# Edge ordering of a two-layer graph network: one-hots and payload laid out with the runs innermost, running sums by scans

## The chip, the cores and the metric

The kernel runs on one core of one Trainium2 chip. The metric is the device time of one execution in microseconds; for each kernel the median of several runs is taken. A core has the engines TensorE (PE; its weight loads are listed as PEld), VectorE (DVE), ScalarE (ACT), GpSimd (POOL) and SyncE (SP, which here issues transfers), each with a queue of its own; they wait for each other by semaphores.

## What is computed

A graph of 12,500 nodes with 128 features and 200,000 edges, sorted by destination (`dst`). First attention over the edges, then three graph convolutions with batch norms, each of which gathers a row per edge by `src`, scales it and sums it by `dst`:

```
h = relu(layernorm(x));  x = x + attention(h, src, dst, edge_attr)
h = relu(layernorm(x))
for W, b, g, beta in three layers:
    h = h @ W
    msg = h[src] * (dinv[src] * dinv[dst])[:, None]
    h = segment_sum(msg, dst) + b
    h = batch_norm(relu(h), g, beta)        # the last layer without relu
x = x + h
```

The part that the change touches computes no feature at all. It orders the edges once, so that the three layers can gather rows of `h` from on-chip memory by small matmuls.

## The kernel before

`build` (L127) calls the stages one after the other: `prepare`, `project`, `attend`, `normalise`, then `arrange` (L1355), then three times `aggregate` and `transform`. `arrange` consists of `survey` (L1381), `rank` (L1530) and `remain` (L1897). Only `rank` is changed.

`rank` takes the edges in 50 spans (`sh.SPANS`) of 28 runs (`SPAN_C`), and a run is 128 edges, one in each partition. The upper part of an edge's source index, its tile, is one of about a hundred. Each span does this:

- SyncE loads the tile numbers of its 3584 edges into `hi_bc`, the same in all partitions (L1611).
- VectorE compares them with the partition's number, `tile_hot` (L1651), which gives the one-hot `oht`. Six halvings (`halve`, L1659) add it up within each run, `count` (L1666) finishes that, and five shifted additions (`add_up`, L1676) turn it into running sums over the 28 runs, `before_c`.
- TensorE compares the edges of a run with each other in seven batches of four runs, `match` (L1810, L1815). ScalarE keeps the earlier ones (L1867). `add_ranks` (L1826, L1829) adds both kinds of count: an edge's rank within its tile.
- VectorE turns ranks into places: `take_rank` (L1683), `test`, `spill`, then five shifted additions over the runs (`run_up`, L1702) that number the edges which found no place, `spill_total` (L1708). TensorE adds the counts of the partitions ahead (`count_ahead`, L1836), ScalarE copies them, and `order_spill` (L1712) to `to_float` (L1750) end in a chunk number and a line number for every edge.
- `chunk_hot` (L1754) makes a one-hot over 29 chunks, `ohc`; `load_pay` (L1763, L1767) multiplies it with two values and a third for five of the chunks, `pay`, 63 columns a run. `line_hot` (L1777) makes the one-hot over 128 lines, `ohw`, one instruction a run.
- `put_down` (L1845) multiplies the two on TensorE, 28 matmuls of 63 columns that add up in one bank, the weights being `ohw`. ScalarE copies the result (L1882, L1884), `turn` (L1852) turns a part of it, and SyncE stores three tables.

The order on each engine is written out by hand, as a list of pairs of a lag and a step that is given to `steps` (L95): in iteration i a step with lag l works on span i - l. VectorE's list (L1793) holds steps of lags 0 to 3, with the short dependent instructions of one span placed between those of another. TensorE's list (L1856) is match 0 to 2 of a span, `count_ahead` of the one before, match 3, `turn` (lag 3), match 4 to 6, `add_ranks`, and last `put_down` with lag 2. Every dependence within an engine goes through a semaphore too. Most tiles have one buffer; `oht`, `before_c`, `tm`, `ohw`, `pay`, `placed` have two.

`pay` and `ohw` have the run as their outer dimension before (`[P, 2, SPAN_C, PAY]`, `[P, 2, SPAN_C, P]`), so a run's 63 or 128 elements are adjacent.

Of the kernel before, what the change touches and what calls it, by code (L numbers as in the profile page):

```python
# [13 lines left out]
P = 128  # L14
# [1515 lines left out]
def rank(nc, sh, env, kept):  # L1530

    with ExitStack() as c:
# [14 lines left out]
        PAD = 16  # L1547
# [4 lines left out]
        sums = [tile(f"sums{k}", [P, PAD + SPAN_C], BF16) for k in range(5)]  # L1552
# [4 lines left out]
        spills = [tile(f"spills{k}", [P, PAD + SPAN_C + 1]) for k in range(6)]  # L1557
# [10 lines left out]
        line_f = tile("line_f", [P, 2, SPAN_C])  # L1568
        ohc = tile("ohc", [P, SPAN_C, PLACE_C], BF16)
        ohw = tile("ohw", [P, 2, SPAN_C, P], BF16)  # L1570
        pay = tile("pay", [P, 2, SPAN_C, PAY], BF16)
# [10 lines left out]
        ident16, iota_col, iota_chunk = kept["ident16"], kept["iota_col"], kept["iota_chunk"]  # L1582
# [7 lines left out]
        summed = [sem(f"summed{k}") for k in range(5)]  # L1590
# [9 lines left out]
        run = [sem(f"run{k}") for k in range(5)]  # L1600
# [35 lines left out]
        @block.gpsimd  # L1636
        def _(pool):
            for k in range(5):
                nc.gpsimd.memset(sums[k][:, :], 0.0)
            for k in range(6):  # L1640
                last = nc.gpsimd.memset(spills[k][:, :], 0.0)
            last.then_inc(padded, 1)

        @block.vector
        def _(dve):
# [125 lines left out]
            def line_hot(q):  # L1771
                def go(s):
# [6 lines left out]
                    if q == 6:  # L1779
                        last.then_inc(ohw_made, 1)  # L1780
# [823 lines left out]
```

## Time and profile before

| | us |
|---|---|
| Median of 3 runs | 6932.62 (6927.31 to 6932.69) |
| The profiled execution, its own time | 6936.31 |
| Its span, first to last instruction | 6934.5 |
| PE busy | 5765.9 (83%) |
| DVE busy | 4671.8 (67%) |
| ACT busy | 2162.6 (31%) |
| POOL busy | 3099.4 (45%) |
| Ordering stage `rank`, first load to last store issued | 3320.45 to 4044.17 |

The page divides the span into 40 slices of 173 us. The ordering stage fills slices 20 to 23: there DVE's digit is 9 or 8, PE's 5 or 6, POOL's 0. In the three layers behind it PE has 9, in attention before it PE has 9 as well. A share of busy time over the whole span is an average over stages with different limits, so the stage is read by itself. TensorE's granted clock is given as a share of its full 2.4 GHz.

### The profile page before, as it was taken

The page shows a single profiled execution, that of the slowest core. Times are in us where ns is not written, and L with a number is a line of the kernel's source. Part 1 is how long each engine was busy: PE and PEld are TensorE (multiplying, and loading weights), DVE is VectorE, ACT ScalarE, POOL GpSimd, SP SyncE. Part 2 cuts the span into 40 slices and gives each one's busy share as a digit, 9 for nine tenths or more (in the row PEclk, how much of TensorE's full clock was granted, in tenths as well). Part 3 has the DMA queues.
Part 4 walks back from the last instruction along what each step waited for, and adds up shares of the span by engine and source line. Part 5 has one row for each costly group of instructions (what it writes and reads, how often), then busy time and mean ns, then how long its engine had stood idle before and what let it go on. Part 6 is the DMA issues. An engine that isn't in the chain of part 4 may idle for free. (4 is left out here: it accounts for less than half of the span.)

```text
span 6934.5 us, 161023 instructions
## 1 busy us (share of the span) xinstructions
PE 5765.9 (83%) x49778; PEld 3934.9 (57%) x49778; DVE 4671.8 (67%) x15150; ACT 2162.6 (31%) x5294; POOL 3099.4 (45%) x3151
## 2 busy tenths in 40 slices
PE   4699999999998999984566659999889999599996
PEld 2466666666666666663344436666456666366664
DVE  7455555555555555558999967777557777577776
ACT  3222222222222222223333323333443333433332
POOL 1555555555555555547000025555145555355552
PEclk9655555555555555555556679999999999799997
DMA  4333333333333333324222233333343333533335
GB/s 145 116 89 87 88 87 88 88 88 89 87 87 87 88 89 86 89 70 131 86 66 70 65 115 105 106 103 104 102 128 104 104 105 101 163 104 106 106 102 152
DMA packets 542000, 688.39 MB, mean 99 GB/s; under 512 B 217072, under 2 KB 427905, under 8 KB 541722
## 3 DMA queue, kind: packets, MB, share of 16 engines
q0 software_dynamic: 140208, 338.71, 17.1%
q1 hardware_dynamic: 401692, 348.45, 16.6%
q8 instruction: 49, 0.80, 0.0%
q14 instruction: 51, 0.42, 0.0%
HBM read 619.25 MB, written 67.52 MB: 99 GB/s over the span
## 5 line engine op out<-in xcount | busy, mean ns | idle before, releaser
L740 POOL DMA_INDIRECT at_kv<-kv_tab,at_idx x1568 | 1562.2, 996 | 1296.6 <-issue 593.6
L2250 ACT ACTIVATE ag_msg<-ag_pair 128x768 bf16<-128x768 f32 x1200 | 925.9, 808 | 1586.4 <-PE ag_pair L2180 1027.1
L2189 PE MATMUL ag_sum<-ag_hot,ag_msg 128*128 128x240 bf16 x10800 | 1300.5, 268 | 69.6 <-issue 55.5
L2189 PEld LDWEIGHTS ag_sum<-ag_hot,ag_msg 128*128 128x128 bf16 x10800 | 974.6, 98 | 443.3 <-issue 366.6
L2064 POOL DMA_INDIRECT ag_spill<-g_tab,ag_idx x600 | 580.1, 967 | 1429.5 <-DMA ag_idx<-spill_tab 777.8
L2119 DVE CAST ag_msg<-ag_pair 128x768 bf16<-128x768 f32 x600 | 572.9, 955 | 588.8 <-PE ag_pair L2180 277.2
L2180 PE MATMUL ag_pair<-xs,ag_pick 128*32 128x384 bf16 x14400 | 821.3, 331 | 153.4 <-DVE ag_pick L2092 63.0
L2071 POOL DMA_INDIRECT ag_spill<-g_tab,ag_idx x750 | 724.5, 966 | 462.3 <-issue 179.1
L2102 DVE TENSOR_SCALAR ag_hot<-iota_win,ag_node 128x240 bf16<-128x240 bf16 x4350 | 901.2, 290 | 0.0
L989 PE MATMUL at_ps_bc<-at_sct,at_sel_head 64*128 64x128 f32 x3136 | 696.8, 408 | 33.9 <-issue 8.2
L989 PEld LDWEIGHTS at_ps_bc<-at_sct,at_sel_head 64*128 64x128 f32 x3136 | 639.2, 308 | 52.0 <-ACT at_sct L1059 41.1
L2180 PEld LDWEIGHTS ag_pair<-xs,ag_pick 128*32 128x32 bf16 x14400 | 305.9, 95 | 476.1 <-issue 251.3
L795 DVE TENSOR_REDUCE at_ml<-at_ps_bc 128x4 f32<-128x512 f32 x392 | 267.6, 690 | 388.3 <-issue 201.4
L1810 PE MATMUL rk_t<-ar_later,ar_negi 128*128 128x512 bf16 x350 | 202.3, 578 | 179.9 <-DVE rk_oht L1651 178.6
L1073 ACT ACTIVATE at_hot_b<-at_ps_turn 128x128 bf16<-128x128 f32 x196 | 54.3, 277 | 891.4 <-PE at_ps_turn L1004 603.7
L1867 ACT ACTIVATE rk_tm<-rk_t 128x512 bf16<-128x512 f32 x350 | 208.4, 597 | 292.3 <-PE rk_t L1815 290.5
L2092 DVE TENSOR_SCALAR ag_pick<-ag_pick,iota_p 128x1024 bf16<-128x1024 bf16 x450 | 217.4, 483 | 101.9 <-DMA ag_pick<-slot_tab 94.2
L776 DVE TENSOR_TENSOR at_prod<-at_ps_q,at_kv 128x512 f32<-128x512 f32 x392 | 252.4, 686 | 48.9 <-issue 30.5
L1045 ACT ACTIVATE at_fall<-at_drop 8x128 f32<-8x128 f32 x196 | 60.5, 309 | 703.9 <-DVE at_drop L845 639.0
L949 PE MATMUL at_ps_q<-at_qd,at_hot_b 64*128 64x512 bf16 x1176 | 253.7, 558 | 12.4 <-DVE at_prod L776 7.7
L2189 PE MATMUL ag_sum<-ag_hot,ag_spill 128*128 128x240 bf16 x2250 | 256.7, 266 | 2.5 <-issue 2.4
L1777 DVE TENSOR_SCALAR rk_ohw<-ar_iota_col,rk_line_f 128x128 bf16<-128x128 bf16 x1400 | 256.4, 246 | 0.0
(331 smaller groups left out, 9093.9 us busy)
## 6 DMA issues: line engine op xcount, KB each, us to landing
ag_pick<-slot_tab SPq DMA_DIRECT2D x150, 768.0 KB
rk_hi_bc<-hi_tab SPq DMA_DIRECT2D x50, 896.0 KB
at_attr<-attr SPq DMA_DIRECT2D x196, 128.0 KB
at_qd<-q_tab SPq DMA_DIRECT2D x1568, 12.0 KB
at_kv<-kv_tab,at_idx POOLq DMA_INDIRECT x1568
ag_spill<-g_tab,ag_idx POOLq DMA_INDIRECT x1350
tr_dv<-dinv_tab SPq DMA_DIRECT2D x72, 256.0 KB
g_tab<-xs SPq DMA_DIRECT2D x48, 384.0 KB
```

The lines of the kernel that those rows point to most:

```text
L740: nc.gpsimd.indirect_dma_start(kv[:, s.slot, ch, :], None, env["kv_tab"], bass.IndirectOffsetOnAxis(ap=idx[:, s.slot, ch:ch + 1], axis=0)) ...
L795: nc.vector.tensor_reduce(ml[:, HALF * j:HALF * (j + 1)], ps_bc[j][:, :].rearrange("p (h e) -> p h e", e=P), AX.X, ALU.max).then_inc(bc_re ...
L949: last = nc.tensor.matmul(ps_q[j][:, :].rearrange("p (c d) -> p c d", d=DIM), hot_b[own, k, :], qd[own, k % 2, HALF * j:HALF * (j + 1), pa ...
L989: last = nc.tensor.matmul(ps_bc[j][:, h * P:(h + 1) * P], sel_head[:, HALF * j + h, :], sct[:, s.slot % 2, :], start=False, stop=h == HALF ...
L1777: last = nc.vector.tensor_scalar(ohw[:, s.slot, ch, :], iota_col[:, :], line_f[:, s.slot, ch:ch + 1], None, ALU.is_equal)
L2064: nc.gpsimd.indirect_dma_start(spill[:, k, o, :], None, table, bass.IndirectOffsetOnAxis(ap=idx[:, k, o:o + 1], axis=0)).then_inc(tail_in[ ...
L2071: nc.gpsimd.indirect_dma_start(spill[:, k, o, :], None, table, bass.IndirectOffsetOnAxis(ap=idx[:, k, o:o + 1], axis=0)).then_inc(spill_in ...
L2102: last = nc.vector.tensor_scalar(hot[:, k, ch, :], env["iota_win"][:, :], node[:, k, ch:ch + 1], None, ALU.is_equal)
L2119: nc.vector.tensor_copy(msg[:, p % 4, :, :], pair_ps[p % 3][:, :, 0:3 * DIM]).then_inc(copied[p], 1)
L2180: last = nc.tensor.matmul(pair_ps[p % 3][at, ch % 2, 0:3 * DIM], pick[:, k, ch * P + j * CAP:ch * P + (j + 1) * CAP], xs[:, (P // CAP) * c ...
L2189: last = nc.tensor.matmul(sum_ps[k][:, 0:WIN], row[:, part * DIM:(part + 1) * DIM], hot[:, k, ch, :], start=first and part == 0, stop=end ...
L2250: nc.scalar.activation(msg[:, p % 4, :, :], pair_ps[p % 3][:, :, 0:3 * DIM], ACT.Copy).then_inc(copied[p], 1)
```

## The change

In `rank` alone:

- A table `iota_x` `[P, 128, 28]` in bfloat16 holds the number of its middle index, the same for all 28 runs. GpSimd writes it once, in front of the stage, and zeroes three small tiles in place of eleven.
- `ohc`, `ohw` and `pay` have the run as their innermost dimension. `line_hot` is 4 tensor-tensor comparisons of 32 lines by 28 runs (896 elements) in place of 28 instructions of 128. `line_f` is bfloat16 in place of float32.
- `chunk_hot` and `load_pay` do the same work with the value of a run broadcast over the middle dimension.
- `put_down` reads a run's weights and columns with a step of 28 elements.
- `count` and the five `add_up` become one `tensor_tensor_scan`, and so do the five `run_up`. Their semaphores and tiles go.
- VectorE's list is written in another order.

```diff
-        sums = [tile(f"sums{k}", [P, PAD + SPAN_C], BF16) for k in range(5)]
...
-        spills = [tile(f"spills{k}", [P, PAD + SPAN_C + 1]) for k in range(6)]
+        spills = tile("spills", [P, SPAN_C])
+        none = tile("none", [P, SPAN_C])
+        queue = tile("queue", [P, SPAN_C + 1])
+        iota_x = tile("iota_x", [P, P, SPAN_C], BF16)
...
-        line_f = tile("line_f", [P, 2, SPAN_C])
-        ohc = tile("ohc", [P, SPAN_C, PLACE_C], BF16)
-        ohw = tile("ohw", [P, 2, SPAN_C, P], BF16)
-        pay = tile("pay", [P, 2, SPAN_C, PAY], BF16)
+        line_f = tile("line_f", [P, 2, SPAN_C], BF16)
+        ohc = tile("ohc", [P, PLACE_C, SPAN_C], BF16)
+        ohw = tile("ohw", [P, 2, P, SPAN_C], BF16)
+        pay = tile("pay", [P, 2, PAY, SPAN_C], BF16)
...
             def count(s):
                 dve.wait_ge(halved[5], s.nth)
-                to = sums[0][:, PAD + 1:PAD + SPAN_C].unsqueeze(2)
-                nc.vector.tensor_tensor(to, halves[5][:, 0:SPAN_C - 1, 0:1], halves[5][:, 0:SPAN_C - 1, 1:2], ALU.add
-                                        ).then_inc(summed[0], 1)
...
+                s.freed(dve, ranked, 2)
+                nc.vector.tensor_tensor_scan(before_c[:, s.slot, 1:SPAN_C], halves[5][:, 0:SPAN_C - 1, 0],
+                                             halves[5][:, 0:SPAN_C - 1, 1], 0.0, ALU.add, ALU.add
+                                             ).then_inc(half_made, 1)
...
+            def run_up(s):
+                dve.wait_ge(spill_made, s.nth)
+                s.freed(dve, over_made, 1)
+                nc.vector.tensor_tensor_scan(queue[:, 1:SPAN_C + 1], spills[:, :], none[:, :], 0.0, ALU.add, ALU.add
+                                             ).then_inc(queued, 1)
...
-                nc.vector.tensor_tensor(ohc[:, :, :], chunk_f[:, :].unsqueeze(2).to_broadcast([P, SPAN_C, PLACE_C]),
-                                        iota_chunk[:, :].unsqueeze(1).to_broadcast([P, SPAN_C, PLACE_C]),
-                                        ALU.is_equal).then_inc(ohc_made, 1)
+                nc.vector.tensor_tensor(ohc[:, :, :], chunk_f[:, :].unsqueeze(1).to_broadcast([P, PLACE_C, SPAN_C]),
+                                        iota_x[:, 0:PLACE_C, :], ALU.is_equal).then_inc(ohc_made, 1)
...
-                nc.vector.tensor_tensor(pay[:, k, :, 0:2 * PLACE_C].rearrange("p c (v m) -> p v c m", v=2),
-                                        ohc[:, :, :].unsqueeze(1).to_broadcast([P, 2, SPAN_C, PLACE_C]),
-                                        kept["vals"][:, :, here(s)].unsqueeze(3).to_broadcast(
-                                            [P, 2, SPAN_C, PLACE_C]), ALU.mult).then_inc(pay_made, 1)
...
+                nc.vector.tensor_tensor(pay[:, k, 0:2 * PLACE_C, :].rearrange("p (v m) c -> p v m c", v=2),
+                                        ohc[:, :, :].unsqueeze(1).to_broadcast([P, 2, PLACE_C, SPAN_C]),
+                                        kept["vals"][:, :, here(s)].unsqueeze(2).to_broadcast(
+                                            [P, 2, PLACE_C, SPAN_C]), ALU.mult).then_inc(pay_made, 1)
...
-                    for ch in range(q * 4, q * 4 + 4):
-                        last = nc.vector.tensor_scalar(ohw[:, s.slot, ch, :], iota_col[:, :],
-                                                       line_f[:, s.slot, ch:ch + 1], None, ALU.is_equal)
-                    if q == 6:
-                        last.then_inc(ohw_made, 1)
+                    at = slice(q * P // 4, (q + 1) * P // 4)
+                    op = nc.vector.tensor_tensor(ohw[:, s.slot, at, :], line_f[:, s.slot, :].unsqueeze(1).to_broadcast(
+                        [P, P // 4, SPAN_C]), iota_x[:, at, :], ALU.is_equal)
+                    if q == 3:
+                        op.then_inc(ohw_made, 1)
...
             steps(dve, sh.SPANS, 2, [
...
+                (1, take_rank), (0, tile_hot), (1, test), (2, line_hot(0)), (1, spill), (0, halve(0)), (1, run_up),
+                (0, halve(1)), (1, spill_total), (0, halve(2)), (2, line_hot(1)), (0, halve(3)), (0, halve(4)),
+                (1, order_spill), (0, halve(5)), (1, differ), (0, count), (1, cut), (3, spill_rows), (1, choose),
+                (2, line_hot(2)), (1, refuse), (2, line_hot(3)), (1, to_int), (1, split), (1, to_float),
+                (1, chunk_hot), (1, load_pay)])
...
-                    last = nc.tensor.matmul(p_ps[k][:, 0:PAY], ohw[:, k, ch, :], pay[:, k, ch, :], start=ch == 0,
+                    last = nc.tensor.matmul(p_ps[k][:, 0:PAY], ohw[:, k, :, ch], pay[:, k, :, ch], start=ch == 0,
```

How the instructions move on VectorE, at two places of one iteration. The rows name line, operation, output and inputs, and elements. First the stretch from the tile one-hot's first halving on, where the running sum over spilled edges is made; before:

```order
L1659 TENSOR_TENSOR rk_half<-rk_oht 128x1792
L1702 TENSOR_TENSOR rk_spills<-rk_spills 128x29
L1659 TENSOR_TENSOR rk_half<-rk_half 128x896
L1702 TENSOR_TENSOR rk_spills<-rk_spills 128x29
L1659 TENSOR_TENSOR rk_half<-rk_half 128x448
L1702 TENSOR_TENSOR rk_spills<-rk_spills 128x29
L1659 TENSOR_TENSOR rk_half<-rk_half 128x224
L1702 TENSOR_TENSOR rk_spills<-rk_spills 128x29
L1659 TENSOR_TENSOR rk_half<-rk_half 128x112
L1702 TENSOR_TENSOR rk_spills<-rk_spills 128x29
L1659 TENSOR_TENSOR rk_half<-rk_half 128x56
L1708 CAST rk_spill_n<-rk_spills 128x1
```

The same stretch in the changed kernel:

```order
L1659 TENSOR_TENSOR rk_half<-rk_oht 128x1792
L1690 SCALAR_TENSOR_TENSOR rk_queue<-rk_spills,rk_none 128x28
L1659 TENSOR_TENSOR rk_half<-rk_half 128x896
L1696 CAST rk_spill_n<-rk_queue 128x1
L1659 TENSOR_TENSOR rk_half<-rk_half 128x448
L1764 TENSOR_TENSOR rk_ohw<-rk_line_f,rk_iota_x 128x896
L1659 TENSOR_TENSOR rk_half<-rk_half 128x224
L1659 TENSOR_TENSOR rk_half<-rk_half 128x112
L1700 TENSOR_SCALAR rk_over<-rk_queue,rk_ahead 128x28
```

The scan is listed as L1690. The count that TensorE waits for (`rk_spill_n`) is made behind the second halving in place of the sixth.

Second, the end of an iteration, from the integer place of an edge to its payload; before:

```order
L1735 CAST rk_slot_i<-rk_slot 128x28
L1736 SCALAR_TENSOR_TENSOR ar_left<-rk_slot,ar_rel 128x28
L1777 TENSOR_SCALAR rk_ohw<-ar_iota_col,rk_line_f 128x128 x4
L1741 TENSOR_SCALAR rk_chunk_i<-rk_slot_i 128x28
L1743 TENSOR_SCALAR rk_line_i<-rk_slot_i 128x28
L1786 SCALAR_TENSOR_TENSOR rk_spill_f<-rk_placed 128x5
L1791 TENSOR_SCALAR rk_spill_i<-rk_spill_f 128x5
L1748 CAST rk_chunk_f<-rk_chunk_i 128x28
L1750 CAST rk_line_f<-rk_line_i 128x28
L1777 TENSOR_SCALAR rk_ohw<-ar_iota_col,rk_line_f 128x128 x4
L1754 TENSOR_TENSOR rk_ohc<-rk_chunk_f,ar_iota_chunk 128x812
L1763 TENSOR_TENSOR rk_pay<-rk_ohc,ar_vals 128x2x28x29
```

In the changed kernel:

```order
L1764 TENSOR_TENSOR rk_ohw<-rk_line_f,rk_iota_x 128x896
L1723 CAST rk_slot_i<-rk_slot 128x28
L1724 SCALAR_TENSOR_TENSOR ar_left<-rk_slot,ar_rel 128x28
L1729 TENSOR_SCALAR rk_chunk_i<-rk_slot_i 128x28
L1731 TENSOR_SCALAR rk_line_i<-rk_slot_i 128x28
L1736 CAST rk_chunk_f<-rk_chunk_i 128x28
L1738 CAST rk_line_f<-rk_line_i 128x28
L1742 TENSOR_TENSOR rk_ohc<-rk_chunk_f,rk_iota_x 128x812
L1750 TENSOR_TENSOR rk_pay<-rk_ohc,ar_vals 128x1624
```

The six short instructions from L1723 to L1738 now stand next to each other, and the last lane one-hot ends ahead of them. TensorE's, ScalarE's and SyncE's lists are as before; on TensorE only the line numbers move.

## Rows read from the trace of the kernel before

**Rows 1.** Windows of the ordering stage: length, busy PE, PEld, DVE, ACT, POOL, PEclk, DMA, GB/s
```profile
3320.00:4060.00 740.00, 457.36 (x6051) 317.20 (x6051) 701.36 (x3359) 248.34 (x550) 0.84 (x11) 0.62 0.23 67
3400.00:3700.00 300.00, 194.10 (x2547) 134.44 (x2548) 292.71 (x1416) 104.13 (x231) 0.00 (x0) 0.61 0.24 68
3456.00:3484.00 28.00, 19.77 (x242) 13.86 (x242) 27.31 (x133) 9.96 (x22) 0.00 (x0) 0.50 0.24 61
```

**Rows 2.** VectorE in order of time, one span of the steady loop (start us, us)
```profile
3598.17 1.14 DVE L1651 TENSOR_SCALAR rk_oht<-rk_hi_bc,iota_p 128x3584 bf16<-128x3584 bf16 x1
...
3601.16 0.18 DVE L1702 TENSOR_TENSOR rk_spills<-rk_spills 128x29 f32<-128x29 f32 x1
3601.28 0.62 DVE L1659 TENSOR_TENSOR rk_half<-rk_half 128x896 bf16<-128x896 bf16 x1
3601.82 0.18 DVE L1702 TENSOR_TENSOR rk_spills<-rk_spills 128x29 f32<-128x29 f32 x1
...
3603.90 0.17 DVE L1676 TENSOR_TENSOR rk_sums<-rk_sums 128x28 bf16<-128x28 bf16 x1
3603.98 0.73 DVE L1777 TENSOR_SCALAR rk_ohw<-ar_iota_col,rk_line_f 128x128 bf16<-128x128 bf16 x4
3604.63 0.16 DVE L1676 TENSOR_TENSOR rk_sums<-rk_sums 128x28 bf16<-128x28 bf16 x1
...
3604.86 0.16 DVE L1676 TENSOR_TENSOR rk_sums<-rk_sums 128x28 bf16<-128x28 bf16 x1
...
3609.11 1.00 DVE L1754 TENSOR_TENSOR rk_ohc<-rk_chunk_f,ar_iota_chunk 128x812 bf16<-128x812 bf16 x1
3610.32 1.85 DVE L1763 TENSOR_TENSOR rk_pay<-rk_ohc,ar_vals 128x1624 bf16<-128x1624 bf16 x1 [0.21 <-DVE rk_ohc L1754]
3612.09 0.31 DVE L1767 TENSOR_TENSOR rk_pay<-rk_ohc,ar_hi 128x140 bf16<-128x140 bf16 x1
3612.31 0.18 DVE L1683 TENSOR_TENSOR rk_rr<-rk_r,ar_rbase 128x28 f32<-128x28 f32 x1
3612.40 1.14 DVE L1651 TENSOR_SCALAR rk_oht<-rk_hi_bc,iota_p 128x3584 bf16<-128x3584 bf16 x1
```

**Rows 3.** Groups of VectorE instructions by line and shape, 3400 to 3900 us
```profile
L1777 DVE TENSOR_SCALAR rk_ohw<-ar_iota_col,rk_line_f 128x128 bf16<-128x128 bf16 x984 | 180.6, 246 | 0.0
L1763 DVE TENSOR_TENSOR rk_pay<-rk_ohc,ar_vals 128x1624 bf16<-128x1624 bf16 x35 | 64.8, 1853 | 7.5 <-DVE rk_ohc L1754 7.5
...
L1659 DVE TENSOR_TENSOR rk_half<-rk_oht 128x1792 bf16<-128x1792 bf16 x36 | 38.9, 1080 | 0.0
L1754 DVE TENSOR_TENSOR rk_ohc<-rk_chunk_f,ar_iota_chunk 128x812 bf16<-128x812 bf16 x35 | 34.9, 998 | 0.0
...
L1659 DVE TENSOR_TENSOR rk_half<-rk_half 128x896 bf16<-128x896 bf16 x35 | 21.9, 625 | 0.0
```

**Rows 4.** TensorE in order of time, one span at the lower clock
```profile
3713.21 0.61 PE L1810 MATMUL rk_t<-ar_later,ar_negi 128*128 128x512 bf16 x1 [2.51 <-DVE rk_oht L1651]
...
3715.41 0.63 PE L1815 MATMUL rk_t<-rk_oht 128*128 128x128 bf16 x4
3717.15 0.18 PE L1836 MATMUL rk_o<-rk_spill_n,ar_before 128*128 128x1 bf16 x1 [1.10 <-DVE rk_spill_n L1708]
...
3722.42 0.17 PE L1829 MATMUL rk_r<-ar_later,rk_tm 128*128 128x1 bf16 x1
3723.28 1.65 PE L1845 MATMUL rk_p<-rk_pay,rk_ohw 128*128 128x63 bf16 x28 [0.69 <-DVE rk_ohw L1777]
```

**Rows 5.** Weight loads of the whole span, by line and shape
```profile
L928 PEld LDWEIGHTS at_ps_max<-at_big_c,at_place 128*128 128x128 f32 x392 | 83.7, 266 | 19.5
```

**Rows 6.** GpSimd instructions of the whole span, by line and shape
```profile
L1457 POOL IOTA iota_win<- 128x240 bf16 x1 | 0.3, 326 | 0.0
...
L1459 POOL IOTA ar_iota_col<- 128x128 bf16 x1 | 0.2, 228 | 0.0
```

**Rows 7.** All engines in order of time, start of the ordering stage
```profile
3324.77 1.15 DVE L1651 TENSOR_SCALAR rk_oht<-rk_hi_bc,iota_p 128x3584 bf16<-128x3584 bf16 x1 [5.16 <-DMA rk_hi_bc<-hi_tab]
```

More of the change, by code:

```diff
@@ L1581, in rank @@
         s_ps = psum("s")
-        ident16, iota_col, iota_chunk = kept["ident16"], kept["iota_col"], kept["iota_chunk"]
+        ident16 = kept["ident16"]
         hi_in = [sem(f"hi_in{k}") for k in range(2)]
@@ L1589, in rank @@
         halved = [sem(f"halved{k}") for k in range(6)]
-        summed = [sem(f"summed{k}") for k in range(5)]
         t_made = [sem(f"t_made{k}") for k in range(BATCHES)]
@@ L1599, in rank @@
              "slots_made"))
-        run = [sem(f"run{k}") for k in range(5)]
+        queued = sem("queued")
         block = c.enter_context(nc.Block())
@@ L1637, in _ @@
         def _(pool):
[L1638 to L1642, printed above, removed]
+            nc.gpsimd.memset(before_c[:, :, :], 0.0)
+            nc.gpsimd.memset(none[:, :], 0.0)
+            nc.gpsimd.memset(queue[:, :], 0.0)
+            nc.gpsimd.iota(iota_x[:, :, :], pattern=[[1, P], [0, SPAN_C]], base=0, channel_multiplier=0,
+                           allow_small_or_imprecise_dtypes=True).then_inc(padded, 1)
         @block.vector
@@ L1693, in spill @@
                 dve.wait_ge(fits_made, s.nth)
-                nc.vector.scalar_tensor_tensor(spills[0][:, PAD + 1:PAD + 1 + SPAN_C], rr[:, :], float(FAR // 2),
+                nc.vector.scalar_tensor_tensor(spills[:, :], rr[:, :], float(FAR // 2),
                                                fits[:, :], ALU.is_lt, ALU.subtract).then_inc(spill_made, 1)
-            def run_up(k):
-                def go(s):
-                    dve.wait_ge(spill_made if k == 1 else run[k - 2], s.nth)
-                    v, d = spills[k - 1], 1 << (k - 1)
-                    n = SPAN_C + 1
-                    nc.vector.tensor_tensor(spills[k][:, PAD:PAD + n], v[:, PAD:PAD + n], v[:, PAD - d:PAD - d + n],
-                                            ALU.add).then_inc(run[k - 1], 1)
-                return go
+            def run_up(s):
[3 more added lines that the diff above has]
+                                             ).then_inc(queued, 1)
             def spill_total(s):
-                dve.wait_ge(run[4], s.nth)
-                nc.vector.tensor_copy(spill_n[:, :], spills[5][:, PAD + SPAN_C:PAD + SPAN_C + 1]).then_inc(spilled, 1)
+                dve.wait_ge(queued, s.nth)
+                s.freed(dve, ahead_made, 1)
+                nc.vector.tensor_copy(spill_n[:, :], queue[:, SPAN_C:SPAN_C + 1]).then_inc(spilled, 1)
             def order_spill(s):
                 dve.wait_ge(ahead_in, s.nth)
-                nc.vector.tensor_scalar(over[:, :], spills[5][:, PAD:PAD + SPAN_C], ahead[:, 0:1],
+                nc.vector.tensor_scalar(over[:, :], queue[:, 0:SPAN_C], ahead[:, 0:1],
                                         float(SLOT_C * P), ALU.add, ALU.add).then_inc(over_made, 1)
```

22 lines of the change are left out of this document (2 added, 20 removed).

## The prediction

> **What bounds the kernel now.** I read the page's 40 slices first. The change touches only `rank`, the ordering stage: it lies between 3320 and 4060 us [rows 1], about 725 of the 6934.5 us of span. The windows of that stage come next [rows 1]: in the second of them VectorE is busy 292.71 of 300 us, TensorE 194.10, ScalarE 104.13, GpSimd 0. The reader should see an engine at 97.6%, and no other above 65%. The order of time on VectorE shows the same from inside [rows 2]: the one-hot of tiles (L1651) begins at 3598.17 and again at 3612.40, so one span of 28 runs costs 14.23 us, and between the two the only idle row is 0.21 us ahead of the payload. A microsecond of VectorE time saved per span is therefore worth 50 us of kernel time, until another chain becomes the longest. The page's own list of costly groups hides this, because attention and aggregation are far longer; their code is not touched.
>
> **What an instruction costs VectorE** is its start to the next start, not its duration, since neighbours overlap by some 0.08 us. Rows for that are in [rows 2], durations by shape in [rows 3]. Bfloat16 tensor-tensor instructions come at two rates there. Those whose every operand runs along adjacent elements (the halvings, L1659): 625 ns for 896 elements and 1080 for 1792, so 0.508 ns an element. Those with an operand broadcast along the innermost dimension (L1754, L1763): 998 ns for 812 and 1853 for 1624, so 1.053 ns an element. The change makes the runs innermost, so that broadcasts lie in a middle dimension.
>
> **The change, part by part, per span.**
>
> *Lane one-hots.* Removed: 7 groups of four L1777, each 0.65 us to the next start (3603.98 to 3604.63 [rows 2]), 4.55 us. Added: 4 instructions of 896 elements. The nearest row has just this size and the fast rate, 0.54 us to the next start (3601.28 to 3601.82), 2.16 us. Gain 2.39. At the slow rate each would take 0.48 us more and the gain would be 0.5: that end is a rival below.
>
> *Chunk one-hot and payload.* By the fast rate 812 elements take 0.58 us in place of 1.00, 1624 take 1.00 in place of 1.85, and 140 some 0.08 less than 0.31. Gain 0.42 + 0.85 + 0.08 = 1.35.
>
> *Running sums.* Removed: five L1702 at 0.12 each (3601.16 to 3601.28), and the first count with five L1676 at 0.08 to 0.12, say 0.10 (3603.90 to 3603.98 is 0.08): 1.2 us. Added: two scans of 27 and 28 elements. The trace has no scan. From below, one costs an L1676, 0.08; from above, as much as the five additions it replaces, 0.60. I take the row of the same length, 0.12, so 0.24 for both: gain 0.96. The Trainium skill ("DVE: opcode table, instruction layouts, handler registers and perf-mode slots", Datapath and trigger behaviour) says that the built-in scan runs at half throughput, which on 28 elements is an estimated 0.03 us each and 3 us on the kernel; no run here shows it yet.
>
> *Waits between neighbours.* Before, a long instruction mostly stood between one that writes and one that reads. Now six short ones in a row (L1723 to L1738 of the change) feed each other at a distance of one or two. A dependent pair with one between stands 0.23 us apart now (3604.63 to 3604.86 [rows 2]), where two free ones take 0.16, so four such places cost some 0.07 each. Together 0.3, between 0 and 0.6.
>
> *VectorE's new span:* 14.23 - 2.39 - 1.35 - 0.96 + 0.3 = 9.83 us.
>
> *TensorE* loses nothing and issues the same instructions, but `put_down` (L1845) now reads both operands with a step of 28 elements, 56 bytes, where it read adjacent ones. One span at the lower clock shows what it needs [rows 4]: from the first match at 3713.21 to the last rank at 3722.59 is 9.38 us, of which 1.10 us were a wait for the spill count (L1836), which VectorE will now hand over right behind the second halving instead of the last. That leaves 8.28. `put_down` spans 1.65 us there, about 52 ns a pair. Since it must follow the ranks and precede the next match, TensorE needs 8.28 + 1.5 = 9.8 us a span at 1.2 GHz (granted 0.50 in the third window of [rows 1]); the stage's mean is 0.62, so often less.
>
> *The price of the step of 56 bytes* is the unknown. From below: 52 ns a pair, as now. From above: as if each weight column cost what it does in the slowest load of 128 columns of that kind, L928, float32, 266 ns [rows 5]. I take the lower end, because these 28 pairs would have to more than double before TensorE is clearly the longest chain. The Trainium skill speaks on both sides. "SBUF — State Buffer" (Specifications) says that SBUF has 16-byte lines and that full bandwidth needs at least two hits on a line, and a step of 56 bytes never gives two. "TensorE: Matmul & The Clock Gate" (Weight-path perf modes) says that fast weight loading of 128 columns takes packed or strided reads. By the second the sum stays; by the first it is the rival of a dear step, and no row of this trace decides.
>
> *A loop through both engines* stands beside these: tile one-hot 1.14, 8.28 on TensorE to the ranks, then L1683 and two waits, 0.3: 9.7 us.
>
> *The front of the stage.* GpSimd now writes a table of 3584 elements before VectorE may start. Its iotas take 326 ns for 240 and 228 for 128 elements [rows 6], 0.875 ns each, so 3.3 us here. VectorE waits 5.16 us for its first load anyway [rows 7], and both begin together, so it costs nothing; without that cover it would be 3 us once.
>
> **The sum.** Three chains of 9.7 to 9.8 us that hand work to each other will not all run without gaps; I allow 0.4 and take 10.2 us. 14.23 - 10.2 = 4.0 us over 50 spans is 200 us. The profiled execution took 6936.3 us (1.8 around its span), the median of the runs shown is 3.7 lower. 6932.6 - 200 = 6733; I say 6735.
>
> **The rivals.**
>
> *The step makes TensorE the bound, still a gain.* At 100 to 150 ns a pair `put_down` takes 2.8 to 4.2 us and the span 11.1 to 12.5 us at 1.2 GHz: 6775 to 6845 us. For it: the line rule above, and that the clock is low in most of the stage. Against it: a denser TensorE may be granted more.
>
> *The step costs more than VectorE gives back.* At 266 ns a pair `put_down` takes 7.45 us, TensorE's span is 8.28 + 7.45 = 15.7 us at 1.2 GHz, and the kernel 50 x 1.5 = 75 us slower: 7008 us. VectorE would then wait for ranks (L1673 of the change). It decides from (14.23 - 8.4) / 28 = 208 ns a pair on. For it: both operands are strided at once. Against it: four times the present price.
>
> *The middle broadcast does not run at the fast rate.* No bfloat16 tensor-tensor row of this trace broadcasts in a middle dimension, so this can't be excluded. Then lane one-hots cost 4 x 1.02 = 4.1 us, chunk and payload gain nothing, and VectorE's span is 14.23 - 0.45 - 0.96 + 0.3 = 13.1: 6877 us. Against it: the halvings read rows of 64, 32 and fewer with jumps between them and keep the fast rate.
>
> *Scans at their upper end:* 0.6 each, 1 us a span more, 6785 us.
>
> **How the numbers follow.** The forecast, a span of 9.5 to 10.6 us: 0.58. The step makes TensorE the bound with a gain: 0.20. Slow broadcast: 0.07. Dear scans: 0.04. The step costs more than it gives: 0.11, of which 0.03 lie within 0.2% of no change, about what a measurement of this kernel can tell from none. So faster by over 0.2% is 0.58 + 0.20 + 0.07 + 0.04 = 0.89, less 0.02 for mishaps unnamed: 0.87; same 0.04; slower 0.09. The range starts at a span of 9.5 us (no waits, higher clock), 6932.6 - 50 x 4.7 = 6697, say 6695. Upward it takes in the dear scans and the whole of the first rival, up to 12.8 us or 157 ns a pair, 6865. It leaves out the slow broadcast and the dear step, 0.18.
>
> **What would show each step.** L1764 at 625 ns and L1742 at 580 confirm the fast rate; 1090 and 998 refute it. L1750 should read 1.0 us. The scans, L1666 and L1690, under 0.22 us. 28 `put_down` pairs (L1830) within 1.7 us confirm the cheap step; 3 us or more is the first rival, 6 or more the second. With the forecast right, VectorE is still above 93% busy in the stage. A stage near 525 us long is the forecast; one above 600 refutes it. If VectorE idles before L1673 or L1700, TensorE's chain is the longer one. Aggregation and attention should keep their lengths within 5 us.

## The result, and the profile after

The changed kernel takes 6731.92 us, the median of 4 runs (6729.05 to 6734.57), against 6931.14 of the kernel before beside it (4 runs, 6927.31 to 6932.69): a ratio of 0.9713, 95% interval 0.9696 to 0.9730, or 199 us less. Forecast were 6735 us and a range of 6695 to 6865. The sum came out by luck: one term of its sum was too low, and two others, too high, covered for it.

The page of the changed kernel, then the windows that answer to [rows 1]:

```profile
span 6731.3 us, 159464 instructions
...
PE 5787.6 (86%) x49778; PEld 4004.8 (59%) x49778; DVE 4457.4 (66%) x13500; ACT 2154.0 (32%) x5294; POOL 3110.5 (46%) x3144
```

```profile
core 0: us, PE busy (x) PEld busy (x) DVE busy (x) ACT busy (x) POOL busy (x), PEclk, DMA share, GB/s
3320.00:3860.00 540.00, 498.57 (x6051) 389.43 (x6051) 480.83 (x1709) 235.91 (x550) 1.29 (x1) 0.73 0.31 91
3400.00:3700.00 300.00, 291.71 (x3531) 228.01 (x3530) 278.35 (x995) 138.25 (x324) 0.00 (x0) 0.75 0.31 91
```

TensorE now is busy 291.71 of 300 us (97.2%), where it was 194.10; VectorE 278.35 (92.8%), where it was 292.71. The two have changed places. TensorE's mean granted clock in the same window rose from 0.61 to 0.75.

How long a span is now, by all 50 tile one-hots:

```profile
L1651 DVE TENSOR_SCALAR rk_oht<-rk_hi_bc,iota_p x50: 1141/1144/1153, 3321.3 to 3818.3; 128x3584 bf16<-128x3584 bf16 x50
```

(3818.3 - 3321.3) / 49 = 10.14 us. The same row before had 3324.8 to 4010.9, so 14.00 (the loop of [rows 2] was a slightly long one). The profiled spans differ by 203.2 us: 189.1 between first and last tile one-hot, 3.5 ahead of the first, 10.6 behind the last, of which 8.1 lie before the last store, where the spans in flight drain at the new speed. The ordering stage runs from 3317.33 to the last store's issue at 3843.50, 526.2 us, where it was 723.7. The other 5.7 us lie outside the stage, in code that was not changed.

VectorE's groups, 3400 to 3800, then its order of time across one span (whole span: 3603.00 to 3613.52):

```profile
line engine op names shapes xcount | busy us, mean ns | idle before us <-releasers
L1764 DVE TENSOR_TENSOR rk_ohw<-rk_line_f,rk_iota_x 128x896 bf16<-128x896 bf16 x157 | 97.0, 618 | 0.0
...
L1750 DVE TENSOR_TENSOR rk_pay<-rk_ohc,ar_vals 128x1624 bf16<-128x1624 bf16 x39 | 39.2, 1005 | 8.6 <-DVE rk_ohc L1742 8.6
...
L1742 DVE TENSOR_TENSOR rk_ohc<-rk_chunk_f,rk_iota_x 128x812 bf16<-128x812 bf16 x39 | 22.7, 582 | 0.0
...
L1700 DVE TENSOR_SCALAR rk_over<-rk_queue,rk_ahead 128x28 f32<-128x28 f32 x39 | 9.4, 240 | 14.0 <-ACT rk_ahead L1859 12.7
...
L1690 DVE TENSOR_TENSOR_SCAN rk_queue<-rk_spills,rk_none 128x28 f32<-128x28 f32 x39 | 8.1, 208 | 0.0
```

```profile
3603.00 1.15 DVE L1651 TENSOR_SCALAR rk_oht<-rk_hi_bc,iota_p 128x3584 bf16<-128x3584 bf16 x1
...
3604.24 0.62 DVE L1764 TENSOR_TENSOR rk_ohw<-rk_line_f,rk_iota_x 128x896 bf16<-128x896 bf16 x1
...
3605.88 0.21 DVE L1690 TENSOR_TENSOR_SCAN rk_queue<-rk_spills,rk_none 128x28 f32<-128x28 f32 x1
3606.01 0.62 DVE L1659 TENSOR_TENSOR rk_half<-rk_half 128x896 bf16<-128x896 bf16 x1
...
3608.62 0.24 DVE L1700 TENSOR_SCALAR rk_over<-rk_queue,rk_ahead 128x28 f32<-128x28 f32 x1 [0.60 <-ACT rk_ahead L1859]
...
3612.36 1.00 DVE L1750 TENSOR_TENSOR rk_pay<-rk_ohc,ar_vals 128x1624 bf16<-128x1624 bf16 x1 [0.22 <-DVE rk_ohc L1742]
...
3613.52 1.14 DVE L1651 TENSOR_SCALAR rk_oht<-rk_hi_bc,iota_p 128x3584 bf16<-128x3584 bf16 x1
```

The lane one-hots, chunk one-hot and payload run at the fast rate in every instance (at most 625, 585 and 1008 ns): 618 ns on average for 896 elements, 582 for 812, 1005 for 1624. A scan lasts 208 ns and takes 0.13 us to the next start. New is the bracket at L1700: VectorE waits up to 0.60 us for the spill count that comes back through TensorE and ScalarE, an idle row that no span had before. In the window 3400 to 3700 this wait and TensorE's longest one are:

```profile
DVE rk_over L1700 <- ACT rk_ahead L1859: 9.7, 21, 0.6
PE rk_t L1795 <- ACT rk_tm L1852: 7.2, 29, 0.3
```

(us in all, times, longest us.) The first is 0.33 us a span, so VectorE's own chain is 10.14 - 0.33 = 9.8 us. The second is for ScalarE; TensorE waits for VectorE nowhere in this window.

TensorE, groups of the same stretch and order of time around two spans' `put_down`:

```profile
L1795 PE MATMUL rk_t<-ar_later,ar_negi 128*128 128x512 bf16 x274 | 140.4, 513 | 10.9 <-ACT rk_tm L1852 9.6
L1800 PE MATMUL rk_t<-rk_oht 128*128 128x128 bf16 x1093 | 140.4, 267 | 0.0
L1830 PE MATMUL rk_p<-rk_pay,rk_ohw 128*128 128x63 bf16 x1097 | 134.2, 295 | 0.0
```

```profile
3601.83 3.40 PE L1830 MATMUL rk_p<-rk_pay,rk_ohw 128*128 128x63 bf16 x28
3605.06 0.60 PE L1795 MATMUL rk_t<-ar_later,ar_negi 128*128 128x512 bf16 x1
...
3612.15 0.16 PE L1814 MATMUL rk_r<-ar_later,rk_tm 128*128 128x1 bf16 x1
3612.17 3.42 PE L1830 MATMUL rk_p<-rk_pay,rk_ohw 128*128 128x63 bf16 x28
3615.42 0.40 PE L1795 MATMUL rk_t<-ar_later,ar_negi 128*128 128x512 bf16 x1
```

The last rank, `put_down` and the next match follow without a gap, and `put_down` no longer waits for VectorE, as it did in [rows 4]. It lasts 3.4 us where it lasted 1.65: (3.40 - 0.295) / 27 = 115 ns a pair, against 52. That is not an effect of the clock, as two windows inside these very groups show:

```profile
3601.90:3605.00 3.10, 3.10 (x31) 3.10 (x29) 3.10 (x9) 0.00 (x0) 0.00 (x0) 0.57 0.67 254
...
3612.20:3615.40 3.20, 3.20 (x33) 3.20 (x30) 3.04 (x9) 0.00 (x0) 0.00 (x0) 1.00 0.89 287
```

Granted 0.57 (mostly 1.2 GHz) the 28 pairs last 3.40 us, granted 1.00 (2.4 GHz) 3.42.

The front of the stage:

```profile
3317.33 5.57 SPq L1611 DMA_DIRECT2D rk_hi_bc<-hi_tab  x3
...
3317.54 3.75 POOL L1641 IOTA rk_iota_x<- 128x3584 bf16 x1
3321.33 1.15 DVE L1651 TENSOR_SCALAR rk_oht<-rk_hi_bc,iota_p 128x3584 bf16<-128x3584 bf16 x1 [4.84 <-POOL rk_iota_x L1641]
```

The iota took 3.75 us, 0.45 more than worked out, and VectorE's wait now ends with it instead of with the load, after 4.84 us where it was 5.16 [rows 7]. Against the kernel before it cost nothing: VectorE begins 4.00 us after the stage's first load is issued, where it was 4.32.

### The profile page after: what moved, and what is told of

It reads as the page before. It is cut to its first block and busy times, and to the rows that moved or that the text cites. A ratio compares the mean times of both kernels' runs of the same rounds, so it can differ in the third digit from the quotient of the medians.

```text
span 6731.3 us, 159464 instructions
## 1 busy us (share of the span) xinstructions
PE 5787.6 (86%) x49778; PEld 4004.8 (59%) x49778; DVE 4457.4 (66%) x13500; ACT 2154.0 (32%) x5294; POOL 3110.5 (46%) x3144
## 5 line engine op out<-in xcount | busy, mean ns | idle before, releaser
L1013 PEld LDWEIGHTS at_ps_scale<-at_we,at_attr 128*128 128x128 f32 x784 | 160.1, 286 | 144.3 <-issue 120.1
L817 DVE TENSOR_TENSOR at_msg<-at_kv,at_msg 128x1024 f32<-128x1024 f32 x196 | 240.3, 1226 | 6.2
```

## The experiments

Two theories were stated. **A**: the step of 56 bytes is dear, TensorE has become the longest chain, and a span lasts as long as TensorE's work in it; that this still gives 3.9 us a span is because the granted clock rose as TensorE grew denser (more of its time busy). **B**: VectorE is still the longest chain, its new span is 9.8 us and waits between neighbours, and the longer `put_down` lies beside it at no cost.

Absolute times differ by chip: the kernel before took 6936.81 us on the chip of the first four runs below and 6878.52 and 6877.13 on that of the others, so versions are compared by their ratio to it, or within a chip.

### What a step costs

Ahead of each real `put_down` (now L1861), 13 groups of 28 pairs go to an unread part of its bank, `ohw` and `pay` read with steps of 1, 2, 4, 7, 14 or 28 elements. Their results are not used.

```diff
+                def stepped(t, k, r, ch):
+                    flat = t[:, k, :, :].rearrange("p e c -> p (e c)")
+                    return flat.rearrange("p (g e r) -> p g e r", g=SPAN_C // r, r=r)[:, ch // r, :, ch % r]
+                for ch in range(SPAN_C):
+                    nc.tensor.matmul(p_ps[k][:, 128:128 + PAY], stepped(ohw, k, 1, ch), stepped(pay, k, 1, ch), start=True, stop=True)
...
```

> The changed kernel, with thirteen extra groups of 28 weight loads and matmuls of 63 columns ahead of put_down in every span, into unused columns of its bank: both operands adjacent, weights alone with a step of 2, 4, 7, 14, 28 elements, columns alone with those steps, both with 4, both with 28. Output as the reference's. Theory A (a step that leaves fewer than two elements in 16 bytes costs extra, as the line rule has it): steps 2 and 4 at some 50 to 55 ns a pair as adjacent reads, steps 7 (14 bytes), 14 and 28 dearer, both with 28 at 115 to 120 ns as put_down showed. Theory B (any step above one element costs the same): step 2 already at 110 ns. Which operand pays is open: if the columns alone, the groups with stepped weights stay at 50 to 55; if the weights alone, the other way round; if both, each below the 115 of the two together. The kernel's time grows by 20 to 35 us a span, 1000 to 1700 us in all.

Measured, in one span (L1835 is both adjacent; L1837 to L1845 the weights at 2, 4, 7, 14, 28; L1847 to L1855 the columns at the same; L1857 and L1859 both at 4 and at 28):

```profile
3628.72 1.04 PE L1835 MATMUL rk_p<-rk_pay,rk_ohw 128*128 128x63 bf16 x28
3629.60 1.05 PE L1837 MATMUL rk_p<-rk_pay,rk_ohw 128*128 128x63 bf16 x28
3630.49 1.10 PE L1839 MATMUL rk_p<-rk_pay,rk_ohw 128*128 128x63 bf16 x28
3631.42 1.66 PE L1841 MATMUL rk_p<-rk_pay,rk_ohw 128*128 128x63 bf16 x28
3632.92 1.64 PE L1843 MATMUL rk_p<-rk_pay,rk_ohw 128*128 128x63 bf16 x24
3634.86 0.38 PE L1843 MATMUL rk_p<-rk_pay,rk_ohw 128*128 128x63 bf16 x4 [0.30 <-issue]
3635.08 1.94 PE L1845 MATMUL rk_p<-rk_pay,rk_ohw 128*128 128x63 bf16 x28
3636.86 1.07 PE L1847 MATMUL rk_p<-rk_pay,rk_ohw 128*128 128x63 bf16 x28
3637.76 1.84 PE L1849 MATMUL rk_p<-rk_pay,rk_ohw 128*128 128x63 bf16 x28
3639.43 3.01 PE L1851 MATMUL rk_p<-rk_pay,rk_ohw 128*128 128x63 bf16 x28
3642.26 3.41 PE L1853 MATMUL rk_p<-rk_pay,rk_ohw 128*128 128x63 bf16 x28
3645.49 3.27 PE L1855 MATMUL rk_p<-rk_pay,rk_ohw 128*128 128x63 bf16 x28
3648.59 1.92 PE L1857 MATMUL rk_p<-rk_pay,rk_ohw 128*128 128x63 bf16 x28
3650.32 3.41 PE L1859 MATMUL rk_p<-rk_pay,rk_ohw 128*128 128x63 bf16 x28
3653.56 3.41 PE L1861 MATMUL rk_p<-rk_pay,rk_ohw 128*128 128x63 bf16 x28
```

Start to next start over 28 gives ns a pair. The columns headed "lines" count the 16-byte lines that the 128 weights, or the 63 columns, touch at that step. The granted clock was not the same for all groups. Two windows, inside the columns at 7 and the columns at 28:

```profile
3639.43:3642.26 2.83, 2.83 (x32) 2.83 (x29) 0.00 (x0) 0.00 (x0) 0.00 (x0) 1.00 0.02 6
...
3645.49:3648.59 3.10, 3.10 (x31) 3.10 (x30) 0.00 (x0) 0.00 (x0) 0.00 (x0) 0.50 0.00 0
```

All groups up to the columns at 7 (L1851) ran at 1.00; the columns at 14 had 0.61, everything behind them 0.50.

| step | weights alone | lines | columns alone | lines |
|---|---|---|---|---|
| 1 | 31 | 16 | 31 | 8 |
| 2 | 32 | 32 | 32 | 16 |
| 4 | 33 | 64 | 60 | 32 |
| 7 | 54 | 112 | 101 | 56 |
| 14 | 62 (1.64 - 0.16 over 24) | 128 | 115 | 63 |
| 28 | 64 | 128 | 111 | 63 |

Both at 4 cost 62 and both at 28 116: the dearer operand sets the price, within 5 ns, and the other hides behind it. So the 63 columns of the payload make `put_down` long, not the weights. A time per line, found from these rows afterwards, fits every row above the floor of 31: 1.8 ns a line for the columns (56 lines 101, 32 lines 58 against 60), 0.5 ns for the weights (112 lines 56 against 54). The Trainium skill ("SBUF — State Buffer", Specifications) gives lines of 16 bytes, and that is the length which fits here. At least two hits on a line, which it asks for full bandwidth, are not enough for the columns at the higher clock, where two hits cost 60 ns, four 32. Why the weights pay less than a third as much for a line is open. Theory A's price for a step of 4, as cheap as adjacent reads, thus held for the weights and not for the columns; the idea that any step costs 110 fell, since a step of 2 costs 32.

The kernel took 8010.84 us in its one run, 1273 more than 0.9713 of the kernel before on that chip. The span is 34.00 us in place of 10.14, so 23.9 more, and the groups take 3653.56 - 3628.72 = 24.8 in this one. The added time shows almost in full, but so much of it would do so under B as well; this run settles the price of a step, not the bound.

### The old sums, in the changed layout

Both scans go, and the ten shifted additions come back between the halvings.

```diff
-                (1, take_rank), (0, tile_hot), (1, test), (2, line_hot(0)), (1, spill), (0, halve(0)), (1, run_up),
...
+                (1, take_rank), (0, tile_hot), (1, test), (1, spill), (2, line_hot(0)), (1, run_up(1)), (0, halve(0)),
+                (1, run_up(2)), (0, halve(1)), (1, run_up(3)), (0, halve(2)), (1, run_up(4)), (0, halve(3)),
+                (1, run_up(5)), (0, halve(4)), (1, spill_total), (0, halve(5)), (2, line_hot(1)), (0, count),
...
```

> The changed kernel with both scans put back as a first addition and five shifted additions each (ten instructions more on VectorE in each span), 1.0 us a span. Theory A (TensorE is the longest chain in the changed kernel, VectorE has 10.14 - 9.4 = 0.7 us of slack a span): only what exceeds the slack shows, 0.3 to 0.5 us a span, 15 to 25 us: 6747 to 6757 us. Theory B (VectorE is still the bound): all of it shows, 45 to 50 us: 6777 to 6782 us.

Measured: 6772.17 us, 0.9770 of before (0.9753 to 0.9786), so 0.0057 or 40 us more than the changed kernel; the span is 10.74 us. Both numbers miss. A's had counted VectorE's slack as all of its 7% idle time, but the 0.22 us ahead of L1750 and its like are VectorE waiting for itself. VectorE's own chain is 9.7 to 9.8 by its wait above and by the kernels with groups below; with the 0.96 us of the sums it is 10.7, which is what was measured. The slack was 0.4 us. Were VectorE the bound all along, as B has it, the span would be 10.14 + 0.96 = 11.1. The 0.60 us that the span grew are 30 us of kernel time; the 40 by the ratio agree with that within the intervals. In this kernel TensorE waits for the spill count again:

```profile
PE rk_o L1839 <- DVE rk_spill_n L1712: 17.6, 23, 1.2
```

### Groups of four runs

Rows of 4 runs innermost, so that `ohw` and `pay` are read with a step of 4 elements. VectorE's work is the same but for one instruction (the payload in two).

```diff
-        ohw = tile("ohw", [P, 2, P, SPAN_C], BF16)
-        pay = tile("pay", [P, 2, PAY, SPAN_C], BF16)
+        ohw = tile("ohw", [P, 2, SPAN_C // R, P, R], BF16)
+        pay = tile("pay", [P, 2, SPAN_C // R, PAY, R], BF16)
...
+            def grouped(t, n):
+                return t.rearrange("p (g r) -> p g r", r=R).unsqueeze(2).to_broadcast([P, SPAN_C // R, n, R])
```

> The changed kernel with the 28 runs in 7 groups of 4: the run within a group is innermost (4 elements), so TensorE reads with a step of 4 elements, 8 bytes, in place of 28, 56 bytes; VectorE's instructions have rows of 4 elements, and the payload of two values is two instructions in place of one. Theory A (TensorE is the longest chain through the dear step, and a step of 8 bytes is cheap): put_down at 1.5 to 1.7 us in place of 3.4, VectorE the bound again with 9.5 to 9.9 us a span, 12 to 32 us faster than the changed kernel: 6700 to 6720 us. Theory B (any step costs the same, or VectorE is the bound anyway): no faster, 6730 to 6740 us, with VectorE's instructions as long as before. If rows of 4 elements cost VectorE its fast rate, L1764 reads 1.0 us and more in place of 0.62 and the kernel is slower, 6850 us or more.

```profile
L1770 DVE TENSOR_TENSOR rk_ohw<-rk_line_f,rk_iota_x 128x896 bf16<-128x896 bf16 x122 | 75.5, 619 | 0.0
...
L1836 PE MATMUL rk_p<-rk_pay,rk_ohw 128*128 128x63 bf16 x868 | 58.5, 241 | 0.0
```

```profile
3400.00:3700.00 300.00, 261.60 (x3718) 190.56 (x3715) 287.94 (x1065) 144.77 (x332) 0.00 (x0) 0.79 0.33 95
```

Those rows are of 3400 to 3700. `put_down` fell to 1.88 us, a little above the 1.5 to 1.7 expected, the span to 9.79, and VectorE (96.0%) is ahead of TensorE (87.2%) again. TensorE now waits for VectorE's tile one-hot in every span, which it never does in the changed kernel:

```profile
PE rk_t L1801 <- DVE rk_oht L1652: 31.0, 30, 1.5
```

The time is 6718.61 us, 0.9690 of before (0.9675 to 0.9705): some 15 us under the changed kernel's ratio, and 0.35 us times 50 is 17. The two intervals overlap, so the ratio alone doesn't decide; the span and the waits do. With only `put_down` shorter the span is shorter: TensorE's chain was the bound, A. VectorE's rows of 4 runs keep the fast rate, 619 ns.

### The kernel before with a denser TensorE

56 more matmuls with adjacent operands, results unused, ahead of `put_down` in the kernel before.

```diff
+                for ch in range(2 * SPAN_C):
+                    nc.tensor.matmul(p_ps[k][:, 128:128 + PAY], ohw[:, k, ch % SPAN_C, :], pay[:, k, ch % SPAN_C, :],
+                                     start=True, stop=True)
```

> The kernel before, with 56 extra matmuls of 63 columns, both operands adjacent, ahead of put_down, into unused columns. Output as the reference's. It asks whether a denser TensorE is granted a higher clock in this stage. TensorE's busy share rises from 0.65 by some 2.8 us a span to 0.80 or more, VectorE stays the bound at 14.2 us a span. Theory A (the density raised the clock from 0.61 to 0.75 in the changed kernel): the granted clock of the stage rises, to 0.68 or more; time within 10 us of the kernel before, 6925 to 6945 us. Theory B (the clock rose for another reason, such as where the stage lies in time): it stays at 0.60 to 0.63.

```profile
3400.00:3700.00 300.00, 216.24 (x3739) 173.85 (x3737) 292.72 (x1409) 101.08 (x231) 0.00 (x0) 0.81 0.23 67
```

Measured: 6937.71 us, 1.0007 of before (0.9997 to 1.0016), span 14.02. In the same 300 us TensorE is busy 216 instead of 194 and its granted clock 0.81 instead of 0.61. So at an unchanged time more matmuls did bring a higher clock here. In the changed kernel the rise has the same direction, but no run isolates its cause there. And in the kernel before neither TensorE's time nor its clock mattered.

### Groups of four and a new order

Against the groups of four, `spill_rows` is cut in two, so that the second half does not wait right behind the first, and the last lane one-hot moves between chunk one-hot and payload.

```diff
-                (0, halve(1)), (1, spill_total), (0, halve(2)), (2, line_hot(1)), (0, halve(3)), (0, halve(4)),
...
+                (0, halve(1)), (1, spill_total), (0, halve(2)), (3, spill_index), (2, line_hot(1)), (0, halve(3)),
+                (3, spill_cut), (0, halve(4)), (1, order_spill), (0, halve(5)), (1, differ), (0, count), (1, cut),
+                (2, line_hot(2)), (1, choose), (1, refuse), (1, to_int), (1, split), (1, to_float), (1, chunk_hot),
+                (2, line_hot(3)), (1, load_pay)])
```

> The kernel with groups of 4 runs, and VectorE's list in another order: the third lane one-hot goes behind the running counts, the fourth between the chunk one-hot and the payload, and the two instructions on the spill rows stand apart, with other work between them. No instruction is added or taken away. Theory A (in the kernel with groups of 4 VectorE is the bound at 9.84 us a span, of which 0.22 are the payload's wait for the chunk one-hot and 0.13 the second spill instruction's wait for the first): both waits go, 0.3 us a span, 15 us: 6700 to 6707 us. Theory B (put_down now starts only when the fourth one-hot ends, 0.6 us later, and TensorE becomes the bound): 6715 to 6735 us.

Measured: 6639.44 us, 0.9656 of before (0.9637 to 0.9675), span 9.41, VectorE busy 297.79 of 300. The wait of 6.8 us in 300 ahead of the payload, 0.22 a span, is gone, and so is one of some 0.13 between the two halves of `spill_rows`. Together they are about the 0.38 us that the span lost.

### The lane one-hots undone

The 28 small instructions return; payload, chunk one-hot and scans stay changed.

```diff
-        ohw = tile("ohw", [P, 2, P, SPAN_C], BF16)
+        ohw = tile("ohw", [P, 2, SPAN_C, P], BF16)
...
+                    for ch in range(q * 7, q * 7 + 7):
+                        op = nc.vector.tensor_scalar(ohw[:, s.slot, ch, :], iota_col[:, :],
+                                                     line_f[:, s.slot, ch:ch + 1], None, ALU.is_equal)
```

> The changed kernel with the lane one-hots as before (28 instructions of 128 elements, four groups of seven, runs outermost), payload and scans as changed: weights adjacent, columns with a step of 28. VectorE gets 2.39 us a span back. Theory A (in the changed kernel TensorE's chain of 10.14 us is only some 0.3 us longer than VectorE's 9.8): VectorE bound at 12.2 us, 2.05 us a span, 100 to 105 us slower than the changed kernel: 6832 to 6837 us. put_down stays at 3.1 to 3.3 us, since the columns alone cost 111 to 115 ns a pair. Theory B (adjacent weights make put_down cheap too): put_down 1.5 to 1.8 us. The time would not tell, VectorE being the bound; the rows do.

Measured: 6773.13 us, 0.9851 of before (0.9833 to 0.9870), span 12.03. It keeps 105 of the 199 us, so undoing the lane one-hots costs some 94 (1.89 us a span), a little less than the 100 to 105 expected. With adjacent weights and strided columns `put_down` still lasts 3.25 us: the columns again.

### Columns alone in groups

As the groups of four, but `ohw` stays as the change has it, with a step of 28.

```diff
-                    last = nc.tensor.matmul(p_ps[k][:, 0:PAY], ohw[:, k, :, ch], pay[:, k, :, ch], start=ch == 0,
+                    last = nc.tensor.matmul(p_ps[k][:, 0:PAY], ohw[:, k, :, ch], pay[:, k, ch // R, :, ch % R], start=ch == 0,
```

> The changed kernel with the payload alone in groups of 4 runs (step of 4 elements for the 63 columns), the weights still with a step of 28. Theory A (the columns make the step dear, the weights cost 64 ns a pair at step 28 and hide behind 60 ns of columns): put_down 1.8 to 2.0 us, VectorE the bound, 6713 to 6724 us, as with both in groups. Theory B (both are needed): put_down 2.5 us or more and 6725 us or more.

Measured: 6661.22 us, 0.9688 of before (0.9670 to 0.9706), span 9.80, `put_down` 1.97 to 1.99 us. (The table has 64 ns for weights at 28 behind columns at 4 with 60.) All that the groups gave comes from the payload's step.

### Groups of two runs

The groups of four with R = 2.

```diff
-        R = 4
+        R = 2
```

> As the kernel with groups of 4, with 14 groups of 2 runs: TensorE's step is 2 elements, 4 bytes. put_down 0.9 to 1.5 us. VectorE's rows have 2 elements. If they keep the fast rate, L1770 reads 0.62 us and the time is that of groups of 4, 6713 to 6724 us, since VectorE is the bound there and TensorE's gain of 0.8 us a span hides behind it. If not, L1770 reads 1.0 us or more and the kernel takes 6780 us or more.

Measured: 6647.87 us, 0.9670 of before (0.9651 to 0.9688), span 9.79. `put_down` is 1.06 or 1.66 us, by the clock, as short as before the change; but VectorE sets the span, which is the same as with groups of four. The interval overlaps theirs. Rows of two bfloat16 elements still run at VectorE's fast rate: 617 ns for 896 elements.

### The changed kernel, and it with the new order alone

The changed kernel unaltered, beside three versions on the same chip; and it with only the table of the new order.

> The changed kernel itself, once more, as the measure for the three kernels beside it on the same chip: 0.971 of the kernel before, a span of the steady loop 10.14 us.

> The changed kernel (step of 28 elements on TensorE) with VectorE's list in the order of the kernel with groups of 4 and fewer waits. That order is worth 0.39 us a span where VectorE is the bound (9.79 to 9.41 us in the traces). Theory A (in the changed kernel TensorE is the bound): the same order brings nothing, a span stays at 10.1 to 10.3 us, the time within 10 us of the changed kernel. Theory B (VectorE is the bound): 0.3 to 0.4 us a span, 15 to 20 us faster than the changed kernel.

Measured: 6677.18 us, 0.9717 (0.9699 to 0.9735), span 10.17, for the changed kernel; 6683.01 us, 0.9725 (0.9708 to 0.9741), span 10.14, with the new order. The order that was worth 0.38 us a span with a step of 4 is worth nothing with 28. What VectorE no longer waits for itself it waits for the count that comes through TensorE. First the changed kernel's wait in 3400 to 3700, then the new order's:

```profile
DVE rk_over L1700 <- ACT rk_ahead L1859: 8.6, 14, 0.6
```

```profile
DVE rk_over L1700 <- ACT rk_ahead L1861: 22.6, 30, 1.0
```

This is the clearest verdict against B.

### The two best candidates side by side

Groups of two, and groups of four once more, both with the new order (diffs as above).

> Groups of 2 runs with the same order. TensorE's put_down takes 1.0 to 1.7 us in place of 1.9, but with groups of 4 and this order VectorE is already busy 99% of the time. Theory A (VectorE bound): a span of 9.36 to 9.42 us, within 5 us of groups of 4 with this order. Theory B (TensorE still holds it up at places, where it waits for the fourth lane one-hot): 5 to 15 us faster than that.

> Groups of 4 with the order of fewer waits, beside the changed kernel on one chip: 0.994 to 0.995 of the changed kernel, 33 to 40 us faster, and 0.966 of the kernel before.

Measured: 6641.49 us, 0.9658 (0.9640 to 0.9675), and 6639.69 us, 0.9653 (0.9637 to 0.9668), spans of 9.43 both. They can't be told apart, since VectorE is busy 297.8 of 300 us in either. The version with groups of four and the new order beats both kernels: 37.5 us (0.994) below the changed kernel on the same chip.

## Why the prediction was right, and which step was wrong

*VectorE's instructions: right.* Expected 625, 580 and 1000 ns, measured 618, 582 and 1005. The rival of a slow middle broadcast fell. The lane one-hots' 2.39 us would be 120 us of kernel time; undoing them costs 94, since part lies behind TensorE's bound.

*Scans: right.* Taken at 0.12 us each, measured 0.12 to 0.13 to the next start. Duration is 208 ns for 28 elements, 26 above the 182 of an addition of 29 in the kernel before. By the half throughput that the Trainium skill ("DVE: opcode table, instruction layouts, handler registers and perf-mode slots", Datapath and trigger behaviour) gives for the scan, it was an estimated 0.03 us more. The trace agrees in the duration; to the next start nothing of it shows.

*VectorE's new span, 9.83: right.* In the changed kernel it is 9.8 without the wait for TensorE's count. The kernel with groups of four, where VectorE is the bound, has 9.79 with one more instruction.

*The price of the step of 56 bytes: wrong.* The text took "the lower end", 52 ns a pair, "because these 28 pairs would have to more than double before TensorE is clearly the longest chain". They did just that: 115 ns, 3.23 us from the last rank to the next match instead of 1.5. The upper bound was taken from a load of weights, 266 ns, and strided weights cost 64 at most; the columns, which do cost, were given no row of their own. The mechanism is the first rival's, TensorE is the bound.

*TensorE's clock: wrong as well, the other way.* The 8.28 us beside `put_down` were read at 1.2 GHz and kept for the whole stage. At the measured mean of 0.75 they take 10.14 - 3.23 = 6.9. With 8.28 the span would have been 11.5 us and the kernel, by the prediction's own arithmetic, 6796: the first rival's range. The prediction had named this against that rival ("a denser TensorE may be granted more") and given it no number. That the clock is what shortened them is read from the trace; no run held it fixed.

*The sum: right by luck, by errors of opposite sign.* 8.28 + 1.5 + 0.4 = 10.2 was forecast, 6.9 + 3.23 = 10.14 came: 1.7 us too little for the step, 1.4 too much for the rest of TensorE's work, and 0.4 for gaps between three equal chains, where there was one longest chain (its idle time, 0.28 us a span, is within the 6.9). The span before was taken as 14.23 us from one loop, where all 50 give 14.00, so the gain between the one-hots was 3.86 us a span and not 4.0; the shorter drain and the 5.7 us outside the stage made up for that in the profiled pair. Of the signs named, "VectorE still above 93% busy" read 92.8%, "3 us or more is the first rival" read 3.4, and the new wait ahead of L1700 was the sign for TensorE's chain. A reader who looks only at the total, or at the stage's 526 us (525 forecast), would have taken the forecast for confirmed.

*The rivals beyond.* The dear step that loses time had to reach 208 ns a pair; it costs 115. The dear scans, 0.6 us each, measured 0.13.

*By parts.* Undoing the lane one-hots costs 94 us, undoing the scans 30 to 40; each is VectorE's time less some 0.4 us a span of its slack. Since that slack counts anew in every such run, the parts do not add up to the 199. Chunk one-hot and payload (67 us forecast, 1.35 us 50 times) were undone in no run; only the durations of their rows bear out their part.

## What to carry to other kernels

When a layout is changed for one engine, price the step that it leaves to the other engine's reads, operand by operand, before the total is trusted: here grouping the runs by four kept all that VectorE had won and gave TensorE back 1.4 us a span. A reordering of VectorE brought nothing while TensorE was the bound (0.9725 against 0.9717), and the same reordering brought 0.38 us a span once VectorE was. And confirm a forecast by the busy share and the waits of each engine, not by the total, which errors of opposite sign can hit.

## What the runs showed that was not expected

- Columns with a step of 28 cost the same at either clock: 3.40 us at a granted 0.57, 3.42 at 1.00. Adjacent ones cost 52 ns a pair at 0.50 and 31 at 1.00. Such a step thus adds most where the clock is high.
- Columns cost some 1.8 ns and weights some 0.5 ns per 16-byte line touched, and the two overlap. A step of 2 bfloat16 elements is all but free in both (32 ns against 31), a step of 4 in the weights (33).
- The busier stretch did not always have the higher clock: 0.81 with TensorE busy 216 of 300 us (the kernel before, denser), 0.86 at 261 and 0.79 at 262 (groups of four, new and old order), 0.75 at 292 (the changed kernel), 0.73 at 292 (the kernel of 13 groups). That last kernel shows it within a span, in each of the six read: with TensorE busy throughout (24.00 of 24.00 us from 3636 on), the clock is 1.00 almost to the end of the columns at 7, falls around the start of the columns at 14, whose mean is 0.50 to 0.61, and is 0.50 in the groups behind them. No run changed the order of the groups, so whether the strided columns are the cause is not shown.
- To the next start, a scan over 27 or 28 elements costs VectorE about as much as one addition of that length (0.12 to 0.13 us against 0.08 to 0.12), so one scan in place of five or six shifted additions saves most of their time.
